# A language-model tower on one core: time terms made in four waves, tables gathered by adding, and a third norm that scales after the centred rows

## The reference, cut to what matters

```python
emb = word + seg + posi + modal + npi + time2vec(age) + time2vec(delay)
#   time2vec(t) = [sin(t*w + b) (191 columns), t*w0 + b0 (1 column)]
h = (emb - mean) * rsqrt(var + 1e-12) * gamma + beta               # first norm
h = h + proj(attention(layernorm(h), 12 heads, q and k rms-normed))  # second norm
x = layernorm(h, eps=1e-5)                                          # third norm
normed = x * rsqrt(mean(x*x) + 1e-6) * ln_w
probs = softmax(normed @ w_router); e = argmax(probs)
y = relu(normed @ wi[e]) @ wo[e]   if the token is among the first 64 of e in its sequence
    else normed
h = h + x + max(probs) * y
```

## Time and profile before

| what | before |
|---|---|
| three runs, us | 479.62, 485.04, 477.85 (median 479.62) |
| the profiled execution's span, us | 484.5 |
| PE busy (share of the span) | 360.7 us (74%) |
| DVE busy | 307.1 us (63%) |
| POOL busy | 252.2 us (52%) |
| ACT busy | 182.4 us (38%) |

### The profile page before, as it was taken

One profiled execution on the slowest core, in us unless ns is written; L12 is line 12 of the kernel. 1 busy time (PEld: TensorE's weight loads), 2 busy tenths in 40 slices (PEclk: granted clock), 3 DMA queues, 4 the chain that ended last, 5 costly groups with the idle time before them and its releaser, 6 DMA issues.

```text
span 484.5 us, 9152 instructions
## 1 busy us (share of the span) xinstructions
PE 360.7 (74%) x3072; PEld 254.6 (53%) x3072; DVE 307.1 (63%) x1002; ACT 182.4 (38%) x372; POOL 252.2 (52%) x294
## 2 busy tenths in 40 slices
PE   0003498898895797897969998620799999999991
PEld 0002385775674766665748766420266556655651
DVE  7266684887989959779566365467256665666540
ACT  1011255454653644644524435210233333333330
POOL 6467546166478366465242222443556657676621
PEclk9999999655868757658575567655699999999997
DMA  5223912011514123215004070597212112212200
GB/s 128 66 49 85 282 25 50 1 28 40 146 43 117 53 65 105 57 49 146 1 18 129 21 202 24 170 304 210 67 30 67 39 49 59 61 44 57 49 18 0
DMA packets 33590, 38.22 MB, mean 79 GB/s; under 512 B 6480, under 2 KB 30777, under 8 KB 33556
## 3 DMA queue, kind: packets, MB, share of 16 engines
q1 hardware_dynamic: 25940, 24.58, 17.9%
q0 software_dynamic: 7040, 12.63, 10.6%
q10 hardware_dynamic: 576, 0.59, 0.4%
HBM read 31.36 MB, written 7.21 MB: 80 GB/s over the span
## 4 chain that ended last, share of the span: by engine, by line
PE 60%; DVE 19%; issue 6%; POOL 5%; DMA 4%; ACT 4%; POOLq 0%; DVEq 0%; ACTq 0%
PE psum L1216 10%; PE psum L1027 9%; PE psum L1028 8%; PE psum L1195 7%; PE psum L1077 5%; PE psum L1200 4%; PE psum L1207 3%; DVE guard L788 3%; POOL weights L358 3%; PE psum L1021 2%; DVE nr_qk L774 2%; PE psum L1022 2%; DMA expert_lists<-tok_col,slot_i 2%; DVE nr_qk L776 2%; DVE rs_qk L778 1%
## 5 line engine op out<-in xcount | busy, mean ns | idle before, releaser
L974 DVE COPY shared<-weights 128x1152 f32 x96 | 69.3, 765 | 16.9 <-issue 10.6
L366 POOL TENSOR_TENSOR small<-small,mhalf 128x2 f32<-128x2 f32 x32 | 25.8, 808 | 76.3 <-DVE small L738 45.0
L456 POOL DMA_INDIRECT tower_out<-shared,oidx x24 | 36.1, 1505 | 40.5 <-DVE shared L988 35.8
L1216 PE MATMUL psum<-shared 128*64 128x192 f32 x576 | 52.1, 330 | 0.9 <-ACT shared L629 0.9
L1027 PE MATMUL psum<-shared,weights 96*128 96x192 f32 (+1 forms) x96 | 48.7, 605 | 3.7 <-ACT weights L507 3.6
L1216 PEld LDWEIGHTS psum<-shared 128*64 128x64 f32 x576 | 39.3, 137 | 19.4 <-issue 13.8
L1028 PE MATMUL psum<-shared,weights 97*128 97x192 f32 (+1 forms) x96 | 44.9, 564 | 0.0
L988 DVE SCALAR_TENSOR_TENSOR shared<-psum,shared 128x192 f32<-128x192 f32 x24 | 10.0, 418 | 47.0 <-PE psum L1216 47.0
L1021 PE MATMUL psum<-ident,weights 128*96 128x128 f32 x16 | 6.6, 413 | 44.1 <-ACT weights L485 43.4
L1195 PE MATMUL psum<-shared 128*64 128x384 f32 x192 | 37.6, 514 | 0.5 <-ACT shared L621 0.5
L1027 PEld LDWEIGHTS psum<-shared,weights 96*128 96x128 f32 x96 | 25.2, 292 | 17.0 <-issue 8.5
(11 more groups left out here) (168 smaller groups left out, 855.4 us busy)
## 6 DMA issues: line engine op xcount, KB each, us to landing
weights<-in_wo SPq DMA_DIRECT2D x16, 576.0 KB, 6.2
weights<-in_wi SPq DMA_DIRECT2D x32, 192.0 KB, 3.9
weights<-in_wi SPq DMA_DIRECT2D x32, 96.0 KB, 4.4
token_rows<-shared SPq DMA_DIRECT2D x14, 192.5 KB
tower_out<-shared SPq DMA_DIRECT2D x14, 96.0 KB
vectors<-in_vectors SPq DMA_DIRECT2D x1, 672.0 KB, 4.7
token_rows<-shared ACTq DMA_DIRECT2D x2, 192.5 KB, 7.4
blk_token<-expert_lists,blk_entry POOLq DMA_INDIRECT x24, 2.5
```

The lines of the kernel that those rows point to most:

```text
L366: G.tensor_tensor(both(src[1]), both(src[0]), mhalf[:, :], ALU.pow).then_inc(sem(done), 1)
L456: G.indirect_dma_start(out=out, out_offset=bass.IndirectOffsetOnAxis(ap=oidx[q % 2][:, :], axis=0), in_=res[q % 2], in_offset=None, bounds ...
L974: V.tensor_copy(w_now[q % 2][k][:, lo:hi], weights[:, bass.ds(at[k] + lo, hi - lo)]).then_inc(sem(("wi_now", "wo_now")[part]), 1)
L1216: last = T.matmul(psum[q % 2][k * BT:(k + 1) * BT, 3, 0:D], hidT[:, c * P + k * BT:c * P + (k + 1) * BT], w_now[q % 2][k][:, WI_COLS + c * ...
```

## The change

It has five parts.

1. **Time terms.** The 16 sequences' arguments come from PE before the turns: a matmul with four rows (two of ones, two of times) against `time_w`, 385 columns, sixteen times, in four waves of four. ACT adds a large constant to round, DVE takes the fraction, ACT the sine (one instruction of 1536 columns a wave), DVE adds age and delay and writes them to `h_all`.
2. **Gathers.** They add onto `h_all` in the DMA (`compute_op=ALU.add`); each waits until the one before it on the same sequence has landed. `sum_terms` and the copy of the ids are gone.
3. **First norm.** DVE does it in two passes, (h - mean)*gamma and then *rstd + beta; ACT's `ln1` and POOL's `scale_shift` are gone.
4. **Third norm.** Both roots come from the variance in one power of four numbers a row. DVE writes the centred rows times ln_w into `row` at once; their scale enters the exponential of the logits and the last factor of the row. ACT's `base_rows` writes h1 + x2 directly, and DVE does `unrouted`.
5. **Loops.** `phase_a` writes all turns out.

```diff
         def phase_a(eng, ahead, turn):
-            for i in range(-ahead, 1):
-                turn(i)
-            with eng.Fori(1, NPAIR - ahead) as i:
-                turn(i)
-            for i in range(NPAIR - ahead, NPAIR):
+            for i in range(-ahead, NPAIR):
                 turn(i)
 # SP
-            load("vectors", tau[:, :, :], t["taus"].rearrange("k p n -> p k n"))
+            load("time", tau_rows[2:4, :], t["taus"])
+            load("time", time_w[:, :], t["time_w"])
...
-            sp.wait_ge(sem("summed"), NSEQ)
+            sp.wait_ge(sem("p_time"), NSEQ // WAVE)
 # POOL
+            def gather_tables(i, parts):
+                for k in parts:
+                    for u, n in seqs(i):
+                        if k == 0:
+                            pool.wait_ge(sem("timed"), n // WAVE + 1)
+                        else:
+                            pool.wait_ge(sem(f"gathered{n}"), 16 * k)
+                        if k == 3 and n == 0:
+                            pool.wait_ge(sem("pair_stored"), 16)
+                        G.indirect_dma_start(
+                            out=h_all[:, n * D:(n + 1) * D], out_offset=None, in_=tables[k],
+                            in_offset=bass.IndirectOffsetOnAxis(ap=ids[:, n, k:k + 1], axis=0),
+                            compute_op=ALU.add,
+                        ).then_inc(sem(f"gathered{n}"), 16)
+            def powers3(i):
+                pool.wait_ge(sem("var3"), i + 1)
+                G.tensor_tensor(pair_small[:, :, RSTD3:RSTD3 + 2], pair_small[:, :, VAR3:VAR3 + 2], mhalf[:, :, :], ALU.pow).then_inc(sem("rstd3"), 1)
             def turn_pair(i):
                 if live(i):
-                    power(i, (MV3 + 1, RSTD3), "var3", "rstd3")
-                    power(i, (SSQ, RSTDN), "ssq_e", "rstdn")
-                    for u, n in seqs(i):
-                        pool.wait_ge(sem("x2"), n + 1)
-                        G.tensor_tensor(row[u][:, D:2 * D], x2[u], h1[u], ALU.add).then_inc(sem("base"), 1)
+                    powers3(i)
                 if live(i + 4):
-                    gather_tables(i + 4, 0, 0)
+                    gather_tables(i + 4, (0, 1))
                 if live(i + 3):
                     embed(i + 3)
                 if live(i + 4):
-                    gather_tables(i + 4, 1, 0)
-                    gather_tables(i + 4, 0, 1)
-                    gather_tables(i + 4, 1, 1)
-                if live(i + 3):
-                    scale_shift(i + 3)
-                if live(i):
-                    unrouted(i, 0)
-                    unrouted(i, 1)
+                    gather_tables(i + 4, (2, 3))
+                if live(i):
                     enlist(i, 0)
                     enlist(i, 1)
 # ACT
+            def sines(w):
+                act.wait_ge(sem("p_time"), w + 1)
+                freed(act, sem("timed"), w - 1)
+                S.activation(waves[w % 2], psum[w % 2][:, :, 0:2 * D], ACT.Identity, bias=round_up[:, 0:1]).then_inc(sem("rounded"), 1)
+            def sines_on(w):
+                act.wait_ge(sem("fraction"), w + 1)
+                S.activation(waves[w % 2], waves[w % 2], ACT.Sin, scale=TWO_PI_BELOW).then_inc(sem("sin"), 1)
+            def base_rows(i):
+                for u, n in seqs(i):
+                    act.wait_ge(sem("nmr3"), i + 1)
+                    act.wait_ge(sem("scale3"), i + 1)
                     freed(act, sem("out_plain"), 64 * i)
-                    normalize(x2[u], h1[u], u, RSTD3, NMR3).then_inc(sem("x2"), 1)
+                    normalize(row[u][:, D:2 * D], h1[u], u, RSTD3, NMR3).then_inc(sem("base"), 1)
 # DVE
+            def fraction(w):
+                dve.wait_ge(sem("rounded"), w + 1)
+                t0 = psum[w % 2][:, :, 0:2 * D]
+                V.scalar_tensor_tensor(waves[w % 2], waves[w % 2], ROUND, t0, ALU.subtract, ALU.subtract, reverse1=True).then_inc(sem("fraction"), 1)
+            def add_times(w):
+                h = h_all[:, w * WAVE * D:(w + 1) * WAVE * D].rearrange("p (n d) -> p n d", n=WAVE)
+                dve.wait_ge(sem("fraction"), w + 1)
+                V.tensor_copy(h[:, :, T2V:D], psum[w % 2][:, :, 2 * D:2 * D + 1]).then_inc(sem("linear"), 1)
+                dve.wait_ge(sem("sin"), w + 1)
+                x = waves[w % 2]
+                V.tensor_tensor(h[:, :, 0:T2V], x[:, :, 0:T2V], x[:, :, D:D + T2V], ALU.add).then_inc(sem("timed"), 1)
+            def third_stats(i):
+                variance(i, lambda u, n: h1[u], "h1", None, STATS3, MV3, None, "3")
+                for u, n in seqs(i):
                     freed(dve, sem("out_plain"), 64 * i)
+                    V.scalar_tensor_tensor(row[u][:, 0:D], h1[u], cols(small[u], MV3, 1), lnw_bc,
+                                           ALU.subtract, ALU.mult).then_inc(sem("normed"), 1)
+                freed(dve, sem("zsum"), 2 * i)
+                V.tensor_scalar(both(VAR3), both(MV3 + 1), NORM_EPS, None, ALU.add).then_inc(sem("var3a"), 1)
+                dve.wait_ge(sem("var3a"), i + 1)
+                V.scalar_tensor_tensor(both(VAR3 + 1), both(VAR3), RMS_EPS, both(MV3 + 1), ALU.mult, ALU.add).then_inc(sem("var3"), 1)
+            def third_scales(i):
+                dve.wait_ge(sem("rstd3"), i + 1)
+                freed(dve, sem("base"), 2 * i)
+                V.scalar_tensor_tensor(both(NMR3), both(MV3), -1.0, both(RSTD3), ALU.mult, ALU.mult).then_inc(sem("nmr3"), 1)
+                dve.wait_ge(sem("nmr3"), i + 1)
+                V.tensor_scalar(both(RSTD3), both(RSTD3), 1.0, None, ALU.add).then_inc(sem("scale3"), 1)
+            def unrouted(i):
+                for u, n in seqs(i):
+                    dve.wait_ge(sem("rp"), i + 1)
+                    dve.wait_ge(sem("base"), n + 1)
+                    V.scalar_tensor_tensor(x2[u], row[u][:, 0:D], row[u][:, 2 * D:2 * D + 1], row[u][:, D:2 * D],
+                                           ALU.mult, ALU.add).then_inc(sem("out0"), 1)
             def turn_pair(i):
                 if live(i):
                     residual(i)
-                    variance(i, lambda u, n: h1[u], "h1", "var3", STATS3, MV3, NORM_EPS, "3")
+                    third_stats(i)
                 if live(i + 2):
                     shift(i + 2, MV2, RSTD2, NMR2, "2")
                 if live(i):
-                    shift(i, MV3, RSTD3, NMR3, "3")
+                    third_scales(i)
...
                 if live(i + 3):
+                    embed_done(i + 3)
                     variance(i + 3, h_of, "h", "var2", STATS, MV2, NORM_EPS, "2")
-                if live(i + 4):
-                    sum_terms(i + 4)
```

249 lines of the change are left out of this document (88 added, 161 removed).

## The result

The changed kernel takes **487.41 us** by the median (five executions, 483.46 to 489.24) against 479.98 for the kernel before (five, 477.85 to 486.18): ratio **1.0122, 95% interval 1.0082 to 1.0163**. That is within 2% of before, but 477 was forecast: the kernel got slower where the forecast had it faster. The profiled execution of the changed kernel has a span of 481.6 us, *shorter* than the 484.5 of before: one pair of profiles does not show what the medians show. So both kernels were profiled a second time (experiments e8 and e11). Their spans are 486.5 and 481.1 us.

A forecast was written before the change was run, and what follows sets the result against it. Bound by three successive stages: start, eight overlapped attention turns, 24 expert tiles; only the first two and the joint change. Terms sum to -2.3 us, 484.5 to 482.2; the same step from the 479.6 median gives 477, range 467 to 491.

The forecast's parts named there:

- start (first guard): Before the turns: first normalised pair at 48.2 us against 42.8, +5.4, and +0.3 at the first guard.
- head norm quiet: Head norm on DVE in the turns: 128x48 operations at 0.21 us once GpSimd's passes go, -12.7 us over eight turns.
- transposes to residual: Back part of a turn: PE's gap shrinks and its transposes run at the higher clock, -6 us, bounds 0 and -8.
- third norm, residual to guard: DVE's extra work between second residual and guard: +1.6 us in each of seven turns, +11.2, bounds +8 and +12.
- guard to attention: PE's 18 us behind the guard: DVE's removed and added passes lie under them, no gain or loss booked.
- joint: Last guard to first expert tile: earlier logits and lists that no longer wait for unrouted, -0.5 us, bounds 0 and -2.3.
- +0.3: Start: pair 2's second power comes at about 69.6 us while the first guard would be due at 69.5.
- Rival 1: Start: slow accumulating gathers; landing at 5 us gives 484, at 7 some 505; decides from 5.7 us, chance beyond that 0.15.
- rival 4: Turns: the quiet head norm is not quiet, +6, 483 us; chance 0.22 together with gathers of 4 to 5.6 us.
- in the place of sum_terms: DVE ahead of the residual: embed_done (1.15 us) replaces sum_terms, the longer by the count of columns; booked at 0.
- rival 2: Start: PE at the higher clock in the waves, passes 0.32 instead of 0.64 us, -5, 472 us; chance alone 0.09.
- Rival 3: Turns: the higher clock reaches into PE's 18 us, two us a turn over seven turns, -14, 463 us; chance 0.12.

The follow-up runs named there:

- e8: The changed kernel again, unchanged, for a second profile: 488.19 us, with the kernel before at 483.29 beside it.
- e11: The kernel before again, unchanged, for a second profile: 482.97 us.
- e1: Changed kernel with gathers that do not add, each still waiting for the one before: 477.97 us.
- e4: Changed kernel; for pair 0 alone GpSimd computes the two powers ahead of pair 1's second and third pair of gathers: 485.37 us.
- e2: Changed kernel with the first expert weights' stream started when pair 1 is normalised instead of pair 0: 485.48 us.
- e5: Kernel before with GpSimd's four tensor operations per sequence beside the head norm narrowed from 192 columns to 2: 463.27 us.
- e12: Kernel before with GpSimd's four operations a sequence and DVE's first two additions of the embedding's terms both narrowed to two columns: 451.53 us.
- e6: Changed kernel with the third norm's centred rows and two scales behind the guard maxima, ScalarE's base rows behind the guards' transposes: 467.84 us.
- e13: Changed kernel with DVE's sum of the unrouted output ahead of the places for all pairs but the last: 487.02 us.

## Why the prediction was wrong

Its sum, term by term, against both pairs of profiles:

| term | forecast | changed less before | e8 less e11 |
|---|---|---|---|
| start (first guard) | +5.7 | +14.4 | +13.6 |
| head norm quiet | -12.7 | -12.4 | -11.9 |
| transposes to residual | -6 | -10.1 | -9.4 |
| third norm, residual to guard | +11.2 | +6.6 | +6.8 |
| guard to attention | 0 | -3.1 | +2.3 |
| joint | -0.5 | +0.5 | +2.6 |
| tiles and end | 0 | +1.1 | +1.3 |
| sum | -2.3 | -2.9 | +5.4 |

The first pair's sum, -2.9, looks like the forecast's -2.3 by luck: a short execution of the changed kernel stands against a long one of before, while the terms themselves are 3 to 9 us off, in both directions. The second pair's +5.4 fits the medians, which are 4.9 apart. The medians miss 477 by 10 to 11 us: 7.7 are the sum (5.4 in place of -2.3), and some 3.5 are the base, 479.6 from three executions of a kernel whose median is 483.

**The start** failed, and it makes the sign: +14 us where 5.7 were booked. The step was "GpSimd next issues pair 1's third and fourth gathers and only then the second power", and the same sum carried on to pair 2: right in order, wrong in price, since an adding issue takes 1.54 us and not 0.95 (e1: 10 us). Two paths end at the first guard, and the prediction had them level: PE's scores of pair 0 behind xn (69.5) and the power behind pair 2's gathers (69.6), hence its +0.3. In the first profile the scores were there at 74.6 us and that power at 79.6. So the guard waits not for xn but for pair 1's power, behind pair 2's last gather at 77.3 us (e4: xn 8 us earlier, the guard 2.5). The weight stream beside pair 2's gathers, which landed in 5.3 to 8.1 us there, is part of that path too (e2: 5.5 us at the guard). My sum "the power until 48.0, xn at 48.2" is what e1 and e4 show, without the adding or with the other order. Rival 1 was the right kind of case (slow adding gathers, other side) with its deciding number on the wrong quantity: the landing never came near 5.7 us outside the stream.

**The quiet head norm** held, as a mechanism and in size, in e5 by itself; rival 4 is out.

**PE's gap and clock**: the size was 3 to 4 us short and the reason half of the truth. I put DVE's additions against embed_done "in the place of sum_terms" at 0; they are 2.4 us against 0.7. Removed alone they give 4, the gap alone 1, both 7 and, in the changed kernel, 9 to 10 us.

**The third norm** held per turn: in five of seven turns the guard stands 1.35 to 1.5 us later behind the residual than before, for the 1.6 booked. The sum is smaller because in two turns of before the guard was later anyway (3.8 and 5.0 us). Set against e12, where that no longer hides so much, the new order costs 9.7 us in the piece. It also makes PE's gap ahead of the guard's transposes 2.5 to 2.7 us in every turn (0.2 to 2.4 before), which the sum had at nothing. e6 takes off 20 us, but it moves more than the change had added, so 20 us is what the place ahead of the guard is worth and not the price of this term.

**The joint** has the wrong sign. The lists do go out earlier behind the guard (by 0.7 to 1.5 us), but the output rows, now behind the places on DVE, go out 1.7 to 2 us later, and the gather of the first tile's tokens takes 5.3 to 6.4 us in place of 2.8 to 3.2. With the rows ahead of the places it took 3.2 (e13). That the gather meets the weight stream, which follows those rows, fits all of this; no run moves the stream alone.

**Rivals.** The waves of PE ran at the slow pace: a pass of 385 columns is 843 ns long, like the 847 ns of a 384-column pass of the projections at the lower level, which has 487 at the higher one. So rival 2 was out. The page's clock row prints 9 there, but the trace's records of the granted clock begin only at 62 us, so that row says nothing of the start. The Trainium skill, page TensorE: Matmul & The Clock Gate, section What's actually happening, has activity release the half clock; these rows do not show it, 10.6 us of passes without a gap kept the slow pace. Rival 3, the higher clock in the 18 us behind the guard, came in part and not always: the same stretch is 3.1 us shorter in one pair and 2.3 longer in the other.

**Open:** the span ends 9.7 us behind the last scatter's issue in the changed kernel and 8.1 in before; no row says why. How the higher clock falls to one turn and not the next was not settled either. Why an adding issue takes GpSimd longer no run shows, only that it does.
